# A decoder layer on one core: rotary tables turned later, queries staged in their own buffer, probabilities and values evicted by halves

## The reference

```
x = layernorm(x + self_attention(x))     # 32 heads of 16, 8 key/value heads, rotary, causal
x = layernorm(x + cross_attention(x, ctx)) # 32 heads of 128, 8 key/value heads, rotary, masked
x = layernorm(x + ffn(x))                # 512x512 product, rows and columns cut by 64 clusters

# cross attention, for each batch b and head h, g = h // 4:
q = rope(x @ Wq)[b, h]; k = rope(ctx @ Wk)[b, g]; v = (ctx @ Wv)[b, g]
p = softmax(where(mask, q @ k.T / sqrt(128), -1e9)); y[b] += (p @ v) @ Wo[h]
```

## Time and profile before

| what | value |
|---|---|
| median of 3 executions | 871.85 us (870.12 to 874.02) |
| profiled execution, its own time | 870.35 us |
| its span, first to last instruction | 868.6 us |
| busy: TensorE, weight loads, VectorE, GpSimd, ScalarE | 779.7, 697.1, 620.9, 404.3, 314.7 us |
| mean granted TensorE clock | 0.971 |
| first stage; second stage; tail | to about 204 us; to about 802 us; to 868.6 us |
| chain that ended last, by engine | TensorE 60%, VectorE 22%, issue 7%, ScalarE 5%, GpSimd 3%, DMA 2% |
| first unit of the second stage | TensorE starts its query and key projections at 215.88 us and ends them at 221.72 us |

### The profile page before, as it was taken

One profiled execution on the slowest core, in us unless ns is written; L12 is line 12 of the kernel. 1 busy time (PEld: TensorE's weight loads), 2 busy tenths in 40 slices (PEclk: granted clock), 3 DMA queues, 4 the chain that ended last, 5 costly groups with the idle time before them and its releaser, 6 DMA issues.

```text
span 868.6 us, 15097 instructions
## 1 busy us (share of the span) xinstructions
PE 779.7 (90%) x5504; PEld 697.1 (80%) x5504; DVE 620.9 (71%) x1108; ACT 314.7 (36%) x590; POOL 404.3 (47%) x422
## 2 busy tenths in 40 slices
PE   3689888898899999999999999999999999997793
PEld 2578777788899888889888898988899898886562
DVE  4478888877686767667667667766666677676768
ACT  3555566653342333233233223333323233322312
POOL 6366666664444535344443435544443454432114
PEclk9699999999999999999999999999999999997997
DMA  9200003012341222123112222212232221121002
GB/s 259 52 17 16 15 15 112 3 53 60 81 131 46 50 73 74 38 64 116 24 48 72 78 55 76 80 24 48 72 97 48 72 72 24 25 85 38 1 1 97
DMA packets 103727, 52.44 MB, mean 60 GB/s; under 512 B 80144, under 2 KB 89488, under 8 KB 103696
## 3 DMA queue, kind: packets, MB, share of 16 engines
q1 hardware_dynamic: 102864, 50.46, 22.3%
q10 hardware_dynamic: 576, 1.05, 0.3%
q0 software_dynamic: 256, 0.52, 0.2%
HBM read 32.62 MB, written 2.10 MB: 40 GB/s over the span
## 4 chain that ended last, share of the span: by engine, by line
PE 60%; DVE 22%; issue 7%; ACT 5%; POOL 3%; DMA 2%; SPq 1%; DVEq 0%; ACTq 0%; POOLq 0%
PE bank L403 22%; PE bank L623 19%; DVE arena_r L1276 10%; PE s_bank L637 4%; PE bank L607 4%; ACT arena_r L821 3%; PE s_bank L639 2%; PE bank L451 2%; PE bank L475 2%; DVE small L1364 2%; DVE arena_f L1358 1%; PE bank L593 1%; PE s_bank L475 1%; ACT arena_f L821 1%; POOL arena_f L1186 1%
## 5 line engine op out<-in xcount | busy, mean ns | idle before, releaser
L403 PE MATMUL bank<-arena_r 128*128 128x256 f32 (+1 forms) x2580 | 356.0, 294 | 1.7 <-DVE arena_r L1276 0.7
L403 PEld LDWEIGHTS bank<-arena_r 128*128 128x128 f32 x2580 | 329.8, 191 | 17.5 <-issue 1.6
L623 PE MATMUL bank<-arena_r 128*128 128x512 f32 x768 | 196.7, 406 | 11.9 <-DVE arena_r L1276 11.9
L821 ACT ACTIVATE arena_r<-bank 128x512 fp32r<-128x512 f32 (+2 forms) x251 | 126.0, 542 | 221.7 <-PE bank L593 83.7
L1276 DVE TENSOR_TENSOR arena_r<-bank,arena_r 128x512 fp32r<-128x512 f32 (+2 forms) x219 | 126.5, 604 | 81.9 <-ACT arena_r L821 80.9
L623 PEld LDWEIGHTS bank<-arena_r 128*128 128x128 f32 x768 | 143.2, 193 | 46.3 <-issue 16.4
L1158 POOL TENSOR_TENSOR arena_f<-arena_f 128x256 f32<-128x256 f32 x64 | 53.9, 842 | 134.4 <-DVE arena_f L1436 133.4
L1186 POOL TENSOR_TENSOR arena_f<-arena_f,small 128x512 f32<-128x512 f32 x32 | 33.5, 1046 | 126.3 <-DVE small L1499 126.3
L821 ACT ACTIVATE arena_f<-s_bank 128x512 f32<-128x512 f32 (+2 forms) x37 | 23.8, 644 | 132.0 <-PE s_bank L639 124.3
L821 ACT ACTIVATE arena_r<-arena_f 128x512 fp32r<-128x512 f32 (+2 forms) x113 | 66.2, 640 | 14.1 <-POOL arena_f L1130 6.1
L1462 DVE TENSOR_TENSOR arena_f<-bank,arena_f 128x512 f32<-128x512 f32 x64 | 43.8, 685 | 38.2 <-PE bank L623 38.2
(11 more groups left out here) (130 smaller groups left out, 1067.9 us busy)
## 6 DMA issues: line engine op xcount, KB each, us to landing
arena_r<-arena_f SPq DMA_DIRECT2D x128, 128.0 KB, 2.5
arena_f<-in_L_xattn_Wq SPq DMA_DIRECT2D x8, 1024.0 KB, 5.5
arena_f<-in_L_xattn_Wo SPq DMA_DIRECT2D x8, 1024.0 KB, 5.6
arena_f<-in_x SPq DMA_DIRECT2D x8, 256.0 KB
arena_f<-in_x SPq DMA_DIRECT2D x1, 2048.0 KB, 15.3
arena_f<-in_L_xattn_Wk SPq DMA_DIRECT2D x8, 256.0 KB, 3.0
arena_f<-in_L_xattn_Wv SPq DMA_DIRECT2D x8, 256.0 KB, 3.3
arena_f<-in_ctx SPq DMA_DIRECT2D x8, 256.0 KB, 3.2
```

The costliest lines, as they stand in the source:

```text
L403: mm = pe.matmul(bank, lhs(a, c), rhs(b, c), start=(c == 0 and n == 0), stop=(c == chunks - 1 and n == 2))
L623: mm = pe.matmul(BO2[i][:], at2[a][:, h, i * P:(i + 1) * P], w2o_s[b][:, h, :], start=(h == 0 and n == 0), stop=(h == HG - 1 and n == 2))
L821: act.activation(dst, src, ACT.Copy).then_inc(done, 1)
```

## The change

1. **Table.** `table_turn` stands behind the first part of the scores of tile 0 and writes banks 3 and 4, four transposes each. ScalarE copies each bank (128 x 512) into a staging place `turned`, between its first two exponents of tile 0. SyncE then issues four DMAs that put the halves into `cosT` and `sinT`. The rotary step of the second stage waits for these (`d_table`), and `pt_stage` of tile 0 waits for the bank that it writes.
2. **Queries.** `stage_q` writes a buffer of its own, `q_st`. It no longer waits for the scores but for the subtractions that read the buffer for the unit before, and is issued a slot earlier (behind the weight loads of SyncE's slot). ScalarE's `q_high` now waits for the scores, and moves ahead of the context's copies and of the exponent. VectorE's `q2_low(u+1, 0)` moves ahead of the context's subtractions and of `total2`.
3. **Halves.** `p_turn` writes half i = 0 to bank 3 and i = 1 to bank 5. `pv` writes i = 0 to banks 6 and 7 and i = 1 to the first halves of banks 4 and 5. The evictions follow by halves: `p2_high` and `p2_low` 2 x 256, `at2_high` and `at2_low` 2 x 256 from banks 6 and 7, then 512 for i = 1 (`second_half`). `out_proj(u, 0)` waits only for i = 0; `scores(u+1)` wait until i = 1 has been read.
4. **Order.** VectorE's `wo_low(g, 3)` moves behind `p2_low`, `values_low` behind `k2_low`, `accumulate(u-1, .., 1)` ahead of the context's subtractions; ScalarE's `k_high` ahead of `v_high`.
5. **Tail.** The last `pv` waits for all four evictions of the transposed ffn weights (`f_wl`), since one of them reads bank 4.

```
@@ buffers
+        q_st = cut(f2.take(HG * 2 * P), j=2, b=4, h=2, q=S)
+        turned = raw[:, 2048:3072]
+        second_half = cut(s_banks, s=2, h=2 * HG, q=S)[:, :, 0:HG, :]
@@ sync
             next_x(2)
+            sp.wait_ge(r_table, 2)
+            for table, half_ in ((cosT, 0), (sinT, S)):
+                for h in range(2):
+                    sp.dma_start(table[S * h:S * h + S, :], turned[half_:half_ + S, :]).then_inc(d_table, 16)
...
             def stage_q(u):
 
+                if not starts_with(u):
+                    sp.wait_ge(c_ql, 2 * u)
                 sp.wait_ge(c_qs, 4 * u + 4)
-                if not starts_with(u):
-                    sp.wait_ge(c_s, u)
...
             def slot(u, g, c):
-                if is_unit(u + 1):
-                    stage_q(u + 1)
...
                     load_o(g + 1)
+                stage_q(u + 2)
...
-            sp.wait_ge(s_qk, 6 * T)
+            sp.wait_ge(s_ex, 4 * T)
             stage_q(0)
             for t in (2, 3):
                 sp.wait_ge(c_xT, t - 1)
                 load_ctx(t)
+            stage_q(1)
@@ tensor
             def table_turn():
 
                 pe.wait_ge(d_cs, 16 * T)
-                for t in range(T):
-                    mm = pe.transpose(s_banks[:, t * P:(t + 1) * P], cs[:, t, :], ident[:])
-                mm.then_inc(r_turn, 1)
+                pe.wait_ge(s_qke, 6)
+                for n in range(2):
+                    for t in range(4):
+                        mm = pe.transpose(banks[3 + n][:, t * P:(t + 1) * P], cs[:, 4 * n + t, :], ident[:])
+                    mm.then_inc(r_turn, 1)
...
-                if isinstance(i, int) and i == 0:
-                    table_turn()
                 if following:
                     pe.wait_ge(s_rq, i + 1)
                     a_stage(i + 1)
-                if isinstance(i, int) and i == 0:
-                    pe.wait_ge(r_table, 4)
                 qk_stage(i, start)
                 s_stage(i, (0, 1), start)
...
+                if start:
+                    table_turn()
                 s_stage(i, (2, 3), start)
...
+            PB2 = (banks[3], banks[5])
...
-                        mm = pe.transpose(TR2[:, (2 * i + h) * P:(2 * i + h + 1) * P],
+                        mm = pe.transpose(PB2[i][:, h * P:(h + 1) * P],
                                           p2[:, (2 * h + i) * P:(2 * h + i + 1) * P], ident[:])
-                mm.then_inc(c_pt, 1)
+                    mm.then_inc(c_pt, 1)
...
                 for i in range(2):
+                    bank = (BO2, BS2)[i]
+                    pe.wait_ge(c_pl, 2 * u + i + 1)
...
-                            mm = pe.matmul(BO2[s][:, 256 * i:256 * i + 256], v2[c % 2][a][rows, i, :],
+                            mm = pe.matmul(bank[s][:, 0:256], v2[c % 2][a][rows, i, :],
...
             def out_proj(u, i):
-                pe.wait_ge(c_al, 2 * u + 2)
+                pe.wait_ge(c_al, 3 * u + i + 2)
...
                 if not first:
-                    pe.wait_ge(c_ad, u)
+                    pe.wait_ge(c_al, 3 * u)
...
             x3_turn(1)
+            pe.wait_ge(f_wl, EC)
             pv(v, v % UN, False)
@@ scalar
-            def table_copy():
-                act.wait_ge(s_w1l, EC + 1)
-                act.wait_ge(r_turn, 1)
-                for table, src in ((cosT, s_banks[0:S, :]), (sinT, s_banks[S:P, :])):
-                    for h in range(2):
-                        copy(table[S * h:S * h + S, :], src, r_table)
+            def table_copy(n):
+                act.wait_ge(r_turn, n + 1)
+                copy(turned[:, 512 * n:512 * n + 512], banks[3 + n][:], r_table)
...
                 expo(i, 0)
+                if not old:
+                    table_copy(0)
+                    table_copy(1)
                 expo(i, 1)
...
             def q_high(u, j):
 
                 act.wait_ge(d_qs, 64 * u + 64)
-                copy(qT2[0][:, j], f32(qT2[1][:, j]), c_qh)
+                if starts_with(u):
+                    act.wait_ge(s_qk, 6 * T)
+                else:
+                    act.wait_ge(c_s, u)
+                copy(qT2[0][:, j], q_st[:, j], c_qh)
...
+            def at2_high(u):
+                act.wait_ge(c_pv, 2 * u + 1)
                 if not starts_with(u):
                     act.wait_ge(c_wo, 2 * u)
+                for s in range(2):
+                    copy(at2[0][:, :, S * s:S * s + S], cut(banks[6 + s][:, 0:2 * P], h=HG, q=S), c_ah)
+                act.wait_ge(c_pv, 2 * u + 2)
+                copy(at2[0][:, :, P:2 * P].rearrange("p h (s q) -> p s h q", s=2), second_half, c_ah)
...
                 corrections(u)
+                if kv_next:
+                    q_high(u + 1, 0)
+                    q_high(u + 1, 1)
                 if turns_ctx(u + 1):
                     ctx_high(2 * c1)
                     ctx_high(2 * c1 + 1)
                 exponents(u)
-                if kv_next:
-                    q_high(u + 1, 0)
-                    q_high(u + 1, 1)
@@ vector
                 masked_max2(u, c)
+                if not starts_with(u):
+                    accumulate(u - 1, (c - 1) % UN, 1)
+                if kv_next:
+                    q2_low(u + 1, 0)
                 if turns_ctx(u + 1):
                     ctx_low(2 * c1)
                     ctx_low(2 * c1 + 1)
-                if not starts_with(u):
-                    accumulate(u - 1, (c - 1) % UN, 1)
                 total2(u)
                 if kv_next:
-                    q2_low(u + 1, 0)
                     q2_low(u + 1, 1)
                 if q_next:
                     rope2_q(u + 2, c2, 0)
                 if c == 0:
                     wo_low(g, 2)
-                    wo_low(g, 3)
                 if kv_next:
                     rope2_k(u + 1, c1, False)
-                p2_low(u)
-                at2_low(u, 0)
-                at2_low(u, 1)
-                if kv_next:
-                    values_low(u + 1, c1)
+                p2_low(u, 0)
+                p2_low(u, 1)
+                if c == 0:
+                    wo_low(g, 3)
+                at2_low(u)
+                at2_low_second(u)
                 if q_next:
                     rope2_q(u + 2, c2, 1)
                 if kv_next:
                     k2_low(u + 1)
+                    values_low(u + 1, c1)
```

79 lines of the change are left out of this document (42 added, 37 removed).

## The result

The changed kernel takes **839.19 us** (median of 4 runs, 838.29 to 841.64), the kernel before, in the same job, 872.93 (4 runs, 870.12 to 874.89): ratio 0.962, 95% interval 0.9584 to 0.9656. The profiled executions span 836.5 and 868.6 us, 32.1 apart; what follows is read from these.

The account below looks back on a forecast made before the run. TensorE was taken to bound the loop. Start 8.1, loop 11.7, first group -2.5 and tail 3.6 sum to 20.9 us: 870.35 becomes 849.45, or 851 us on the median's scale; range 842 to 860.

Parts of the forecast that it names:

- The floor of the loop: Loop: TensorE, busy 71.85 of 74.70 us a group, bounds it; only some 2.85 us idle can be won.
- The wait of 0.34: Ordinary units, before the output projection: TensorE's wait for evictions goes through halves in separate banks, 0.34 us each.
- c = 0: First unit of a group: waits of 1.65 and 0.17 us go, GpSimd's keys' sum costs 0.2; gain 1.6 us.
- c = 2: Third unit of a group: queries land late, their copies delay the exponent; loses 0.65, gains 0.33, net loss 0.3 us.
- The start: First head transposes no longer wait for the rotary table: at about 22.3 instead of 30.45 us, gain 8.1 us.
- The first group: Units 0 to 3: queries' copies ahead of the context's delay the key projection; loss 2.5 us, 0.7 of it for clock.
- The tail: Last group and end: gains at c = 0 and in the last units, together 3.6 us, bounds 1 and 7.
- Nothing new waits: Whole kernel: DMA lands early, c = 2 and GpSimd's chain cost nothing, tail keeps its clock; 844 us, chance 0.17.
- GpSimd becomes the bound of c = 0: Keys' transpose at c = 0 waits 1.1 instead of 0.2 us, in seven units; 857 us, chance 0.10.
- the slower one: All units: queries land late and delay exponent and probabilities in 31 units; 888 us, chance 0.04.
- the one by which the change does nothing: Halves wait for each other through shared counters or banks, only the start is won; 863 us, chance 0.04.
- the reading that was put against the second: GpSimd's addition beside VectorE's SBUF work: stretched by 0.45 us (1.18 against 0.73 alone), not blocked for a full 0.91 us subtraction.

Follow-up runs that it names:

- experiment 1: The kernel before with only the halves of probabilities and attended values, evicted from separate banks: 845.7 us, ratio 0.9704.
- experiment 10: The kernel of experiment 7 with VectorE subtracting the second half of the attended values twice and the output projection waiting for it: 858.8 us, ratio 0.9843.
- experiment 8: The kernel before with only the attended values in halves, the probabilities transposed and evicted whole: 852.8 us, ratio 0.9767.
- experiment 6: The changed kernel with GpSimd making the queries' second sum before the first weight subtraction in units c = 1: 832.4 us, ratio 0.9524.
- experiment 2: The kernel before with only the table change, turned behind the first scores and copied to its halves by DMA: 862.4 us, ratio 0.9902.
- experiment 5: The changed kernel with its queries as before (old buffer, copied behind the exponent, both subtractions behind the sum): 831.0 us, ratio 0.951.
- experiment 7: The changed kernel with queries' copies behind the exponent and both subtractions behind the sum in c = 2, first three and last three units: 827.7 us, ratio 0.9465.
- experiment 3: The kernel before with only the queries change (own buffer, early load, copies ahead of the exponent, first subtraction ahead of the sum): 875.4 us, ratio 1.0054.

## Why the prediction was wrong in size

**The floor of the loop: the step that failed.** "TensorE bounds the loop, and its idle time, some 2.85 us a group, is all that an edit can win there", and "TensorE waits 0.34 us for them ... The wait of 0.34 goes". The place was right, the wait went, and nothing took its room; the size was not. The wait at the output projection was worth 0.61 in each unit (experiment 1), since the idle time shown starts at a modelled end that runs 0.25 us over the start of the work behind it (experiments 1 and 10), and since the probabilities' halves give 0.13 where no wait is shown (8). A group takes 71.5 us, 3.2 less instead of 1.95, and lies below the 72.1 at which the prediction calls itself wrong. Over the six groups the profiles differ by 20.3 us (24.95 - 4.69) instead of 11.7: 6 x 3.2 = 19.2, and 1.1 from a stretch at a lower granted clock that only the kernel before has, which is chance. The loop is 8.6 of the 11.2 us by which the profiles go beyond the forecast, the tail 3.6, the first group 1.1, and the first stage takes 2.0 off; the medians add 1.6.

**c = 0** gained 1.99, forecast 1.6. The wait of 1.65 at the probabilities times values, worth 1.71, is gone, and so is that of 0.17 at the output projection, worth 0.42 (0.55 us from the transposes' start, 0.13 without a wait). Late next is the keys' sum on GpSimd, as forecast: it ends at 299.78 and the transposes that need it start at 299.92, 0.11 later in the unit than at c = 1. The unit is 0.15 above the ordinary one, where 0.2 were forecast.

**c = 2.** Forecast a loss of 0.3 (wait 0.65 minus the gain 0.33); measured a loss of 0.1. The mechanism is the one predicted, to the instruction: a weight subtraction ahead of the sum, the DMA late, the copies ahead of the exponent (experiment 6). TensorE waits:

```profile
617.58 0.44 PE L607 MATMUL bank<-ident,arena_f 128*128 128x128 f32 x2 [0.48 <-POOL arena_f L1212]
```

Here too the price is 0.72 (18.38 against 17.66), not the 0.48 shown.

**The start** was right: forecast 22.3 and 8.1 us, measured 22.17 and 8.3, and alone worth 8.5 in the median. That it fits to 0.1 us is partly luck: in the six profiles of kernels that share this first stage (the change, experiments 2, 5, 6, 7 and 10) it comes anywhere from 21.91 to 23.63. The 2.2 us lost to the clock in one profile are not a term of the change.

**The first group**: forecast a loss of 2.5 us. From the last tile's head transposes, 6.1 earlier, to the output projection of unit 3, 4.7 earlier, the change loses 1.4. The wait for the key projection was sized well (4.12 in experiment 3, "4.1" forecast). Experiment 5 splits the rest: without the queries' own buffer this stretch is 4.3 us shorter than before, and with it 1.4 longer, so the queries cost 5.7 and halves and order gave back 4.3. The forecast did not price these apart, so which of them was off is not shown. The 0.7 us that were added for the clock did not show (1.00 over units 0 to 3, from 218 us on).

**The tail**: forecast 3.6 us, measured 7.2 (32.1, the span, less the 24.95 at unit 27). Halves alone give 4.6 in the last four units. The queries' late landing in unit 30 is as predicted (wait of 3.22 for 1.58 in the earlier trace rows); behind it the projection takes 3.76 us where it took 5.46:

```profile
760.27 0.44 PE L607 MATMUL bank<-ident,arena_f 128*128 128x128 f32 x2 [3.22 <-POOL arena_f L1212]
...
763.85 3.76 PE L638 MATMUL bank<-arena_r 128*128 128x512 f32 x12
```

At least 1.7 us of the tail are so the clock, which the prediction kept out of its sum. From unit 30 to 31 the changed kernel takes 17.2 us at a granted clock of 0.95, experiments 5 and 7, with the same matmuls there, 18.1 at 0.84 and 19.3 at 0.77. The Trainium skill, TensorE: Matmul & The Clock Gate, "What's actually happening", says that how many matmuls run slow differs between runs of one kernel. The runs agree as far as they can: the four executions of experiment 5's kernel have mean granted clocks of 0.978 to 0.988 and spans of 831.7 to 826.2 us.

**The rivals.** "Nothing new waits" is nearest in time (844), but not in cause: something new waits, and the floor it rests on (71.85) is undercut. "GpSimd becomes the bound of c = 0" fell, with 0.15 us where it had 1.1; so did the slower one and the one by which the change does nothing. But the reading that was put against the second, that the trace shows a stretching and no lock, was wrong. The lock is there (last section). A loser waits for the rest of the other's instruction, and as it comes when that is about half done, the wait looks like a stretching by half.

## What to carry to other kernels

A wait of a pipelined engine costs the difference from start to start against the same place without a wait; the idle time that a profile shows leaves out the overlap of the modelled end (0.25 and 0.08 us here, by place), and the busy time with waits in it is no floor. Price a change that hastens the bottleneck with its other waits at the new pace: the queries' early copy cost nothing in the loop before, and 0.7 us a group behind the halves. A copy whose input comes by DMA belongs ahead of an in-order engine's urgent work only where the input is surely there; elsewhere the same buffer pays with the copy behind it. Before an instruction is taken out of VectorE's order, look at what GpSimd runs at the place where the next one lands.
